# The four parts of a sample 32 partitions apart instead of in neighbouring ones

## What is computed

```
h    = silu(cond @ W1.T + b1)            # (128, 512)
gate = sigmoid(h @ W2.T + b2)[:, None, :]
a    = inverse_haar(gate * haar(x))      # the transform is over the 128 steps
out  = x + (x + a)
```

## Time and profile before

| | |
|---|---|
| time, median of 3 runs | 166.81 us (166.54 to 166.82) |
| the profiled execution | 166.82 us |
| its span, first to last instruction | 165.1 us |
| VectorE busy | 80.0 us (48%), 20 instructions |
| TensorE busy (matmul) | 22.7 us (14%), 68 matmuls |
| ScalarE, POOL busy | 2.5 us, 2.6 us |
| moved by DMA | 69.47 MB, mean 421 GB/s |

### The profile page before, as it was taken

The page is one execution under the profiler, slowest core; times in us unless marked ns, Lnnn a source line. Parts: engine busy times, 40 slices in busy tenths (PEclk is TensorE's granted clock), DMA queues, the critical chain, the costliest instruction groups (busy, mean ns, idle before and its releaser), DMA issues.

```text
span 165.1 us, 219 instructions
## 1 busy us (share of the span) xinstructions
PE 22.7 (14%) x68; PEld 12.2 (7%) x68; DVE 80.0 (48%) x20; ACT 2.5 (2%) x3; POOL 2.6 (2%) x10
## 2 busy tenths in 40 slices
PE   0099969800000000000000000000000000000000
PEld 0093722300000000000000000000000000000000
DVE  0052380499999999999970000000004999700000
ACT  3000100100000000000000000000000000000000
POOL 6000000000000000000000000000000000000000
PEclk9999987995555555555555555555555555555555
DMA  5999969969998997989997996999899799799995
GB/s 151 474 456 508 476 286 508 508 286 476 508 397 365 508 508 254 508 349 413 508 429 334 508 508 302 461 508 413 349 508 445 334 492 508 318 445 405 445 421 254
DMA packets 1732, 69.47 MB, mean 421 GB/s; under 512 B 194, under 2 KB 194, under 8 KB 324
## 3 DMA queue, kind: packets, MB, share of 16 engines
q1 hardware_dynamic: 1008, 43.25, 61.4%
q10 hardware_dynamic: 724, 26.22, 36.9%
HBM read 35.92 MB, written 33.55 MB: 421 GB/s over the span
## 4 chain that ended last, share of the span: by engine, by line
DMA 50%; DVE 19%; PE 12%; DVEq 5%; ACT 1%; issue 0%
DMA ring<-in_x 23%; DMA out<-ring 22%; DVE ring L242 10%; DVE ring L247 5%; DVEq L30 5%; DMA ring<-in_L_cond_W 5%; PE gate_sum L173 3%; PE turned L181 2%; PE hidden_sum L151 2%; PE turned L135 2%; DVE ring L229 2%; PE hidden_sum L146 1%; PE turned_cond L140 1%; DVE factor L237 0%; DVE ring L222 0%; ACT ring L193 0%
## 5 line engine op out<-in xcount | busy, mean ns | idle before, releaser
L242 DVE TENSOR_TENSOR ring<-ring,factor 128x16384 f32<-128x16384 f32 x3 | 51.5, 17220 | 0.0
L247 DVE TENSOR_TENSOR ring<-ring,factor 128x8192 f32<-128x8192 f32 x2 | 17.3, 8688 | 40.5 <-DMA ring<-in_x 40.5
L216 DVE COPY ring<-turned 128x512 f32<-128x512 f32 x4 | 2.8, 692 | 10.0 <-PE turned L135 10.0
L237 DVE TENSOR_SCALAR factor<-turned 128x512 f32<-128x512 f32 x4 | 2.8, 691 | 6.9 <-PE turned L181 6.9
L173 PE MATMUL gate_sum<-ring 128*128 128x512 f32 x8 | 5.4, 833 | 1.3 <-DVE ring L227 1.3
L135 PE MATMUL turned<-identity,ring 128*128 128x128 f32 x16 | 3.6, 423 | 8.4 <-DMA ring<-in_L_cond_W 8.4
L229 DVE COPY ring<-turned 128x512 f32<-128x512 f32 x4 | 3.9, 1056 | 0.0
L135 PEld LDWEIGHTS turned<-identity,ring 128*128 128x128 f32 x16 | 3.3, 227 | 8.4 <-issue 8.4
L181 PE MATMUL turned<-ring 128*128 128x512 f32 x8 | 3.7, 601 | 0.8 <-ACT ring L193 0.8
L151 PE MATMUL hidden_sum<-ring 128*128 128x512 f32 x8 | 3.7, 605 | 0.0
L222 DVE TENSOR_TENSOR ring<-hidden_sum,ring 128x512 f32<-128x512 f32 x1 | 0.7, 692 | 5.6 <-ACT ring L190 5.6
(11 more groups left out here) (17 smaller groups left out, 6.6 us busy)
## 6 DMA issues: line engine op xcount, KB each, us to landing
out<-ring ACTq DMA_DIRECT2D x2, 4096.0 KB, 20.8
ring<-in_L_cond_W ACTq DMA_DIRECT2D x1, 1024.0 KB, 7.7
ring<-in_L_cond_W SPq DMA_DIRECT2D x1, 1024.0 KB, 7.5
ring<-in_cond SPq DMA_DIRECT2D x1, 256.0 KB, 7.7
ring<-in_x SPq DMA_DIRECT2D x3, 34.6
b_row<-in_L_cond_b ACTq DMA_DIRECT2D x2, 2.0 KB
out<-ring SPq DMA_DIRECT2D x2, 45.6
ring<-in_x ACTq DMA_DIRECT2D x1, 38.6
```

The source lines that it names most:

```text
L216: dve.tensor_copy(w1_t[:, c, :], turned[c][:, :]).then_inc(w1_t_set, 1)
L242: dve.tensor_tensor(ring[:, c, :, :], ring[:, c, :, :], steps_of(c, STEPS), ALU.mult).then_inc(chunk_scaled, 1)
L247: dve.tensor_tensor(ring[:, 0, piece(h), :], ring[:, 0, piece(h), :], steps_of(CHUNKS - 1, PIECE), ALU.mult).then_inc(chunk_scaled, 1)
```

## The change

The order of the two indices inside the partition dimension is turned round: h is outside and q inside, so partition = 32 h + q. The four parts of a sample are then 32 partitions apart, and neighbouring partitions hold the same part of neighbouring samples, 256 KB apart in DRAM. The pattern of a chunk in DRAM keeps h and q as two dimensions. The matrix `spread` has its ones where sample = 32 g + partition mod 32, and is made by a memset to zero and one select. `chunk` and the last stores take one more index.

```diff
+    Q = B // GROUPS
-    x_parts = x.rearrange("(g q) (h n) d -> g (q h) n d", g=GROUPS, h=GROUPS)
-    out_parts = out.rearrange("(g q) (h n) d -> g (q h) n d", g=GROUPS, h=GROUPS)
+    x_parts = x.rearrange("(g q) (h n) d -> g h q n d", g=GROUPS, h=GROUPS)
+    out_parts = out.rearrange("(g q) (h n) d -> g h q n d", g=GROUPS, h=GROUPS)
...
-        spread = ring[:, SCRATCH, 22:22 + GROUPS, 0:P]
+        spread = ring[:, SCRATCH, 22:22 + GROUPS, 0:P].rearrange("s g (h q) -> s g h q", q=Q)
...
-            return parts[c // PER_GROUP, :, r * STEPS:(r + 1) * STEPS, :]
+            return parts[c // PER_GROUP, :, :, r * STEPS:(r + 1) * STEPS, :]
...
-            pool.memset(spread, 1.0).then_inc(ones_spread, 1)
-            pool.wait_ge(ones_spread, 1)
-            pool.affine_select(out=spread, in_=spread, compare_op=ALU.is_ge, fill=0.0, base=0,
-                               pattern=[[P, GROUPS], [1, P]], channel_multiplier=-GROUPS).then_inc(lower_set, 1)
-            pool.wait_ge(lower_set, 1)
-            pool.affine_select(out=spread, in_=spread, compare_op=ALU.is_ge, fill=0.0, base=GROUPS - 1,
-                               pattern=[[-P, GROUPS], [-1, P]], channel_multiplier=GROUPS).then_inc(spread_set, 1)
+            pool.memset(spread, 0.0).then_inc(zeros_spread, 1)
+            pool.wait_ge(zeros_spread, 1)
+            pool.affine_select(out=spread, in_=spread, compare_op=ALU.not_equal, fill=1.0, base=0,
+                               pattern=[[Q, GROUPS], [0, GROUPS], [1, Q]], channel_multiplier=-1).then_inc(spread_set, 1)
...
-                pe.matmul(spread_gate[g][:, :], spread[:, g, :], gate, start=True, stop=True).then_inc(gate_spread, 1)
+                pe.matmul(spread_gate[g][:, :], spread[:, g, :, :].rearrange("s h q -> s (h q)"), gate, start=True, stop=True).then_inc(gate_spread, 1)
...
-                act.dma_start(chunk(out_parts, CHUNKS - 1)[:, piece(h), :],
+                act.dma_start(chunk(out_parts, CHUNKS - 1)[:, :, piece(h), :],
                               ring[:, 0, piece(h), :]).then_inc(done[h], DMA_DONE)
```

More of the change, by code:

```diff
@@ L74, in gated_residual_program @@
         hidden_turned, hidden_t_set = sem("hidden_turned"), sem("hidden_t_set")
-        ones_spread, lower_set, spread_set = sem("ones_spread"), sem("lower_set"), sem("spread_set")
+        zeros_spread, spread_set = sem("zeros_spread"), sem("spread_set")
         gate_summed, gate_set = sem("gate_summed"), sem("gate_set")
```

## The result

The changed kernel takes 922.68 us (median of 6 runs, 915.57 to 927.5) beside 166.81 us (166.54 to 167.01) for the kernel before: 5.530 times as long, 95% interval 5.520 to 5.541. The profiled execution took 924.66 us, its span is 922.8 us. That lies inside the range of the prediction, but at neither of its two main cases (637 us, and 1108 to 1265 us).

A forecast was written before the change was run, and what follows sets the result against it. The prediction took bytes per DMA engine as the bound: 632.7 us of work on each of four engines plus 2.8 us head and tail gave a 635.5 us span, 637.2 us time; range 620 to 1275 us.

The forecast's parts named there:

- two main cases: Four engines at their present rate, 637 us, chance 0.42; four engines in pairs at one SBUF port, 1108 to 1265 us, 0.38.
- What bounds the kernel: Whole kernel: bytes per DMA engine bound it, with the queues' packets filling 98.3% of the 16 engines' time.
- Four engines: Nine large transfers: DRAM outer count 4 against 128 gives four engines; small packets fall from 194 to 86.
- The rate of an engine: Large transfers: a busy engine keeps 26.75 GB/s, so 16.92 MB on each of four takes 632.7 us.
- The order and the cover: Queues and waits: x0 lands near 86 us, gate chain and VectorE passes stay off the path, engines work without a gap.
- POOL, TensorE, the issues: One POOL select (0.63 us) goes, hidden; TensorE passes unchanged; nine issues take a few tenths more, at most 1 us.
- two engines at one door: Rival: rows 32 partitions apart share one SBUF entry at one engine's rate; about 1108 to 1265 us, chance 0.38.
- Something else than four: Rival: two or one engine (1265 us to 2.5 ms), or drifting pairs (650 to 1108 us); chance 0.08.
- The claim that engines keep step: Argument for paired engines sharing an SBUF entry throughout: neighbours that start together stay together, read from bunched packet ends.
- sixteen engines: Rival: large transfers keep 16 engines, about 167 us, no difference; chance 0.12.

The follow-up runs named there:

- two engines that never meet: Changed kernel with two groups in place of four, so two DMA engines work on partitions 0 to 63 and 64 to 127; 1247.8 us.
- the head start: Changed kernel with two small DRAM copies (51 and 17 rows of 16 KB) ahead of x0, setting one engine of each pair 10 us behind; 655.89 us.
- the control: Changed kernel with one copy of 68 rows of 16 KB ahead of x0, holding up all four engines alike; 935.7 us.
- the run with two queues and sixteen engines: Changed kernel with each large transfer cut into four parts, parts 0 and 1 on SP's queue, 2 and 3 on ACT's; 272.63 us.

## Why the prediction was right or wrong, point by point

**What bounds the kernel** held: DMA before, and DMA after, now four engines at 0.25 of 16.

**Four engines** held exactly. 86 small packets and 1624 in all were foretold, and the counts of 68 with an outer count of 2, 3 + 1 with 51 and 17 rows, and 626 with 32 follow the same rule. The reading of the packet counts in the earlier trace rows was enough to see that the number of engines goes with the shape; that it would be four came from an argument, which the runs bore out.

**The rate of an engine** was the term that failed. The sum took the 26.75 GB/s that an engine has when 16 work on 16 different places, and carried it over to four that work in pairs on the same one. For the part that isn't shared it was close: two engines that never meet have 27.1 GB/s, so that the forecast would have been about 1% lower still. With the head start four engines took 655.89 us, of which some 20 us are the two copies ahead of x0 on engine 0: that is the forecast's sum. What it left out is the sharing, 297 us by the table and 280 us by the control against the head start.

**The order and the cover** held in kind: no compute work is on the path, the gate chain ends where it did (SP issued x2 at 33.19 us), and the four engines hardly rest. The landing times were off by the rate: x0 at 166 us instead of 86.

**POOL, TensorE, the issues** cost nothing, as said. POOL is busy for 2.0 us instead of 2.6. One issue, ACT's of out2, held its queue for 2.21 us, more than the few tenths I allowed, behind a transfer of 171 us.

**The rival "two engines at one door"** had the right mechanism. Its first size, 1265 us, took the sharing as total; in x0 it nearly is (158 us, near the 157 foretold). Its second, 1108 us, let the stretch of x3 and out1 run at full rate, and with 100 GB/s it nearly did; that a load and a store don't hinder each other at an entry, the reason given, isn't shown. What neither size has is that the engines of a pair don't stay in step, so that each later stretch of the table costs less than the one before up to out1: some 185 us between 1108 and 923. The prediction did name this, as an argument against the rival ("once one of two leads by a few rows they no longer meet") and under "Something else than four" as "a pair of engines drifting apart, 650 to 1108 us". It worked out no sum for it and gave it 0.04. So the measured time fell where the prediction had put little, and its range held it because it spanned both main cases: that part is luck. The claim that engines keep step, read from the packets that end in bunches in the earlier trace rows, held for one row after another but not over a transfer: after x0 the pairs were 1.5 to 1.8 us apart, after out0 6 us.

**The rival "sixteen engines"** fell with the first count of packets. Its remark that nothing priced the distance in DRAM is now answered, for one dimension of 128 rows, with at most half a per cent.

## What to carry to other kernels

The order of a transfer's dimensions decides how many DMA engines it gets: look at the outermost count of both sides, and at the number of small completion packets in the profile. Here a view that couldn't merge its first two dimensions fell from 128 to 4, and the time rose 5.5 times with the same bytes in runs of the same length. If a layout needs such an order, find one whose outermost dimension is the whole of the partitions; cutting the transfer by parts got the engines back but not their separate places in SBUF (297 us).

Engines that are all busy can still be at half their rate. A DMA share near 1 with half the GB/s of another stretch is the sign for that, and moving stores beside loads, or one of the engines by some microseconds, can tell whether they stand in each other's way.

## What the runs showed of the hardware that I had not expected

Two engines that share an entry drift apart by themselves, by 1 to 2 us per transfer of 32 rows each, until they are about four rows apart and no longer meet. That is why the changed kernel speeds up from 53 GB/s in x0 to 75 in out0; the 100 after that also need the load beside the store. Why the engine ahead gains stays open.

Issuing instructions can block. With two engines, SP's issue of x2 held its queue for 120 us, and each of the four-engine kernels issued x2 in half a microsecond:

```profile
33.21 120.13 SPq L105 DMA_DIRECT2D ring<-in_x  x1
```

With 64 rows per engine in each transfer, x0 and x1 were in the queue ahead of it; it returned at 153 us, when x0 was nearly through. Nothing waited for it there, but whatever SP had to issue next would have. It isn't only a matter of few engines: in the run with two queues and sixteen engines SP's six issues of x0, x1 and x2, in pieces, took 62.93 us together. What limits an issue wasn't tried.

```profile
1.66 62.93 SPq L98 DMA_DIRECT2D ring<-in_x  x6
```
